# One pipeline for the state space and rotary stages, and another order of work in the latent attention

## The reference, cut to what matters

```python
# state space: a circulant map W (diagonal in Fourier space) steps the state
h_t = W h_(t-1) + B_w u_t              # u = layernorm(x)
x   = x + C_w h_t + D * u
# last layer, on x' = layernorm(x):
h   = x' + attention(rms_norm(x', norm1_w))    # rope on its input, causal softmax
x   = x + h + moe(rms_norm(h, norm2_w))        # router: top 2 of 8 experts
def rope(v):                                    # cos, sin by position in the sequence
    xe, xo = v[..., 0::2], v[..., 1::2]
    return concat([xe * cos - xo * sin, xe * sin + xo * cos])
```

## Time and profile before

| what | us |
|---|---|
| median of the runs (of 3, 1023.49 to 1028.31) | 1025.85 |
| the profiled execution, its own time | 1029.01 |
| its span, first to last instruction | 1027.2 |
| PE busy in the span | 787.1 |
| DVE busy | 540.1 |
| POOL busy | 439.3 |
| ACT busy | 428.7 |

### The profile page before, as it was taken

The page is one execution under the profiler, slowest core; times in us unless marked ns, Lnnn a source line. Parts: engine busy times, 40 slices in busy tenths (PEclk is TensorE's granted clock), DMA queues, the critical chain, the costliest instruction groups (busy, mean ns, idle before and its releaser), DMA issues.

```text
span 1027.2 us, 21336 instructions
## 1 busy us (share of the span) xinstructions
PE 787.1 (77%) x7200; PEld 574.0 (56%) x7200; DVE 540.1 (53%) x1413; ACT 428.7 (42%) x1491; POOL 439.3 (43%) x637
## 2 busy tenths in 40 slices
PE   2899997799789477999966526776545999999980
PEld 1677775688644135777744315564432566666660
DVE  3477876468644345788865764765231323322323
ACT  1577775256524124676651023666102333333320
POOL 4566663525377768777733343354350000000005
PEclk9899999789889788999996756876557999999995
DMA  8322225613332545554410003132392065152004
GB/s 277 144 73 77 78 59 190 217 48 110 99 123 73 185 131 169 168 168 136 145 42 0 0 0 123 43 97 89 106 379 72 27 236 179 38 197 87 17 22 123
DMA packets 66198, 116.82 MB, mean 114 GB/s; under 512 B 6576, under 2 KB 22704, under 8 KB 65456
## 3 DMA queue, kind: packets, MB, share of 16 engines
q1 hardware_dynamic: 57936, 105.25, 31.0%
q10 hardware_dynamic: 6624, 6.03, 1.8%
q0 software_dynamic: 1536, 4.20, 1.3%
HBM read 81.11 MB, written 34.34 MB: 112 GB/s over the span
## 4 chain that ended last, share of the span: by engine, by line
PE 51%; DVE 16%; POOL 10%; ACT 9%; issue 8%; DMA 4%; ACTq 0%; SPq 0%; DVEq 0%; POOLq 0%; another core or an unknown queue 0%
ACT probs L1208 6%; PE ps L622 5%; PE ps L1046 4%; PE ps L1047 4%; PE ps L1048 4%; PE ps L638 3%; PE ps L520 2%; PE ps L662 2%; PE ps L1069 2%; PE ps L1071 2%; PE ps L1070 2%; PE ps L522 2%; PE ps L521 2%; DVE probs L1712 2%; PE ps L1058 2%
## 5 line engine op out<-in xcount | busy, mean ns | idle before, releaser
L1393 POOL TENSOR_TENSOR piece_out<-piece_in,piece_out 128x512 f16<-128x512 f32 x96 | 117.0, 1219 | 7.7
L1611 POOL DMA_INDIRECT pt<-y_rows,neg x16 | 15.3, 959 | 233.3 <-DMA y_rows<-vbuf 228.7
L2145 DVE TENSOR_TENSOR probs<-ps,ctx_t 128x512 f32<-128x512 f32 x46 | 29.6, 686 | 154.0 <-PE ps L1048 154.0
L1358 POOL TENSOR_TENSOR var<-mv,half 128x1 f32<-128x1 f32 x48 | 9.3, 194 | 186.1 <-DVE mv L1627 114.3
L622 PE MATMUL ps<-pack_const,probs 128*128 128x128 f32 x512 | 75.4, 281 | 4.6 <-issue 3.1
L1392 POOL CAST piece_out<-piece_in 128x512 f16<-128x512 f32 x96 | 62.7, 653 | 24.0 <-DMA piece_in<-in_w 23.5
L1046 PE MATMUL ps<-arena,qbuf 128*128 x184 | 70.7, 384 | 0.0
L1047 PE MATMUL ps<-arena,qbuf 128*128 x184 | 70.5, 383 | 0.0
L1048 PE MATMUL ps<-arena,qbuf 128*128 x184 | 70.3, 382 | 0.0
L622 PEld LDWEIGHTS ps<-pack_const,probs 128*128 128x128 f32 x512 | 58.0, 143 | 21.1 <-issue 15.0
L1149 ACT ACTIVATE probs<-probs,mx 128x256 f32<-128x256 f32 x128 | 63.1, 498 | 6.9 <-DVE mx L1712 6.9
(11 more groups left out here) (286 smaller groups left out, 2192.8 us busy)
## 6 DMA issues: line engine op xcount, KB each, us to landing
piece_in<-in_w SPq DMA_DIRECT2D x96, 256.0 KB, 2.9
w_parts<-piece_out SPq DMA_DIRECT2D x96, 256.0 KB, 2.1
arena<-w_parts SPq DMA_DIRECT2D x8, 3072.0 KB, 12.8
ctx_t<-in_ctx SPq DMA_DIRECT2D x32, 256.0 KB, 2.9
x_rows<-piece_out SPq DMA_DIRECT2D x1, 2944.0 KB, 17.7
qbuf<-x_rows ACTq DMA_DIRECT2D x23, 128.0 KB, 2.1
y_rows<-vbuf ACTq DMA_DIRECT2D x23, 128.0 KB, 1.7
arena<-in_xa SPq DMA_DIRECT2D x2, 1282.0 KB, 7.8
```

Source lines behind the costliest of these rows:

```text
L1393: pool.tensor_tensor(both[:, PIECE:], src, both[:, 0:PIECE], ALU.subtract).then_inc(piece_split, 1)
```

## The change

- `ssm` and `rope` become one pipeline without a hardware loop. PE takes tile `k-4` of `rope` behind tile `k-2` of `ssm`. The scaling, the four products and the joining of `rope` move from DVE to POOL (`multiply`, `join_turns`), with `norm1` multiplied into the tables once. The root is no longer applied to the rows: ACT writes a diagonal matrix of it (`root_diagonal`), and the transposing product on PE is made with that matrix in place of the identity.
- D * u is no longer computed on POOL: ACT writes a diagonal of D, and PE adds two products of `XT` with it into the same PSUM tile (`read_out`). `keep_rows` and the copy into `xs` go away. PSUM tiles of the stage are doubled.
- `la` gets its own order on every engine, four slots for values, and `row_maxima` waits for the transposes of the tile whose buffer it overwrites.
- The router's products of tile `k-5` are made inside the steps of `la` (`route_rows`).

The diff, cut to its core:

```diff
-                    hold(pe, g["pt_copied"], 2 * (i - 2) + 1)
+                    hold(pe, g["pt_copied"], 2 * (i - (2 if st == "sa" else 3)) + 1)
...
+                def route_rows(i):
+                    if i == 0:
+                        pe.wait_ge(*loaded["moe"])
+                    hold(pe, g["xt"], i + 1)
+                    hold(pe, g["shifted"], at_most(i + 5, TILES))
+                    for c in range(DC):
+                        last = pe.matmul(S[:, 768 + i * 8:768 + (i + 1) * 8], tile_of_x(i, c),
+                                         kc(W["moe"]["router_w"], 8)[:, c, :], start=c == 0, stop=c == DC - 1)
+                    if i == TILES - 1:
+                        last.then_inc(prep_mm, 1)
...
+                for k in range(INNER_STEPS if st == "la" else 0):
+                    if live(k, 3, TILES):
+                        mix_values(k - 3)
+                    if live(k, 0, TILES):
+                        project(k)
+                    if live(k, 3, TILES):
+                        join_heads(k - 3)
+                    if live(k, 5, TILES):
+                        route_rows(k - 5)
+                    if live(k, 0, TILES):
+                        values(k)
+                        score(k)
+                    if live(k, 2, TILES):
+                        turn_probs(k - 2)
+                    if live(k, 4, TILES):
+                        turn(k - 4)
...
-                def project(i, s):
-                    hold(pe, g["x_copied"], i + 1)
-                    hold(pe, g["rotated"], i)
...
+                def read_out(i):
                     hold(pe, g["modulated"], i + 1)
-                    hold(pe, g["resid"], i)
+                    hold(pe, g["resid"], i - 1)
+                    if i == 0:
+                        pe.wait_ge(d_spread, 2)
                     for c in range(DC):
-                        last = pe.matmul(M[:, 256:512], rot2[:, s * D + c * P:s * D + (c + 1) * P],
-                                         kc(cg[:, :], D)[:, c, :], start=c == 0, stop=c == DC - 1)
+                        pe.matmul(state_out[i % 2], rot2[:, (i % 2) * D + c * P:(i % 2) * D + (c + 1) * P],
+                                  kc(cg[:, :], D)[:, c, :], start=c == 0, stop=False, skip_group_check=True)
+                    for c in range(DC):
+                        last = pe.matmul(state_out[i % 2][:, c * P:(c + 1) * P], XT[:, c, i * P:(i + 1) * P],
+                                         d_diagonal[:, c * P:(c + 1) * P], start=False, stop=True, skip_group_check=True)
                     last.then_inc(g["projected"].sem, 1)
-                def step(k, s, h):
+                def turn_rope(i):
+                    r = G["rope"]
+                    hold(pe, r["roped"], i + 1)
+                    hold(pe, r["weighed"], i + 1)
+                    hold(pe, r["xt"], i)
+                    for c in range(DC):
+                        last = pe.matmul(C[:, c * P:(c + 1) * P], rope_rows[i % 2][:, c * P:(c + 1) * P],
+                                         root_diagonal[i % 2], start=True, stop=True)
+                    last.then_inc(r["turned"].sem, 1)
...
+                for k in range(TILES + 4):
                     if live(k, 1, TILES):
-                        sum_over_time(k - 1, 1 - s)
+                        sum_over_time(k - 1)
                     if live(k, 0, TILES):
-                        project(k, s)
+                        project(k)
                     if live(k, 2, TILES):
-                        out(k - 2, s)
-                skewed(pe, TILES, 2, step)
-            if "rope" in RUN:
-                g = G["rope"]
-                def step(k, s, h):
-                    hold(pe, g["roped"], k + 1)
-                    hold(pe, g["xt"], k)
-                    for c in range(DC):
-                        last = pe.transpose(C[:, c * P:(c + 1) * P], rot[:, c * P:(c + 1) * P], ident)
-                    last.then_inc(g["turned"].sem, 1)
-                skewed(pe, TILES, 0, step)
+                        read_out(k - 2)
+                    if live(k, 4, TILES):
+                        turn_rope(k - 4)
...
+                for k in range(INNER_STEPS if st == "la" else 0):
+                    if live(k, 1, TILES):
+                        exps(k - 1, range(HEADS))
+                    if live(k, 2, TILES):
+                        copy_probs(k - 2)
+                    if live(k, 3, TILES):
+                        square(k - 3)
                     if live(k, 4, TILES):
-                        i = k - 4
-                        hold(act, g["turned"], i + 1)
-                        act.activation(XT[:, :, i * P:(i + 1) * P], C[:, 256:512].rearrange("p (c n) -> p c n", c=DC),
-                                       ACT.Copy).then_inc(g["xt"].sem, 1)
-                        if st == "la":
-                            act.activation(row_parts[i % 2][:, (i // 2) * 2 * D:(i // 2) * 2 * D + D], xn[:, :], ACT.Copy)\
-                               .then_inc(g["row_hi"].sem, 1)
+                        copy_rows(k - 4)
+                        take_high(k - 4)
...
+                def multiply(i):
+                    hold(pool, g["normed"], i + 1)
+                    hold(pool, r["roped"], i)
+                    pairs = tile(xn_all, i).rearrange("p (n a) -> p n a", a=2)
+                    for j, odd in enumerate((0, 1, 0, 1)):
+                        last = pool.tensor_tensor(xs[:, j * P:(j + 1) * P], pairs[:, :, odd], rope_tables[:, j * P:(j + 1) * P],
+                                                  ALU.mult)
+                    last.then_inc(r["multiplied"].sem, 1)
+                def join_turns(i):
+                    hold(pool, r["multiplied"], i + 1)
+                    hold(pool, r["turned"], i - 1)
+                    rows_out = rope_rows[i % 2]
+                    pool.tensor_tensor(rows_out[:, 0:P], xs[:, 0:P], xs[:, P:2 * P], ALU.subtract)
+                    pool.tensor_tensor(rows_out[:, P:2 * P], xs[:, 2 * P:3 * P], xs[:, 3 * P:4 * P], ALU.add)\
+                        .then_inc(r["roped"].sem, 1)
+                for k in range(TILES + 4):
+                    if live(k, 3, TILES):
+                        multiply(k - 3)
+                    if live(k, 3, TILES):
+                        hold(pool, r["weighed"], k - 4)
+                        inverse_root(r, k - 3, 2, mv[:, 0:1], "squared", "rooted", rstd2[:, (k - 3) % 2:(k - 3) % 2 + 1])
                     if live(k, 2, TILES):
-                        root_of_variance(g, k - 2)
+                        i = k - 2
+                        inverse_root(g, i, 1, mv_pair[:, 2 * (i % 4) + 1:2 * (i % 4) + 2], "stats", "rstd",
+                                     rstd_pair[:, i % 4:i % 4 + 1], omega)
+                    if live(k, 3, TILES):
+                        join_turns(k - 3)
...
+                    if st == "la":
+                        hold(dve, g["p_turned"], 2 * i - 2)
...
+                for k in range(INNER_STEPS if st == "la" else 0):
+                    if live(k, 1, TILES):
+                        sum_values(k - 1)
+                        row_maxima(k - 1, (k - 1) % 2)
+                    if live(k, 3, TILES):
+                        gather_outputs(k - 3)
+                    if live(k, 0, TILES):
+                        copy_queries_and_keys(k)
+                    if live(k, 2, TILES):
+                        scale_probs(k - 2, k % 2)
+                    if live(k, 3, TILES):
+                        add_heads(k - 3)
+                    if live(k, 4, TILES):
+                        scale_rows(k - 4)
+                    chain.restart()
```

233 lines of the change are left out of this document (107 added, 126 removed).

## The result

Four runs of the changed kernel have a median of **979.63 us** (979.10 to 981.45), four of the kernel before beside them 1027.05 us (1023.49 to 1028.31): a ratio of **0.9547, 95% interval 0.9518 to 0.9576**. The forecast was 984.0 in 974 to 1001. The profiled execution of the changed kernel took 979.1 us, with a span of 977.0; the span before was 1027.2, so the profiles differ by 50.2 us.

A forecast was written before the change was run, and what follows sets the result against it. No engine was full; rings of waits between engines, one per tile, and a second rotary pass bounded the kernel. Gains of 12.4 and 29.5 us made 41.9, from 1029.0 to 987.1, less 3.2 for the median: 984, range 974 to 1001.

The forecast's parts named there:

- The start does not move.: First pipeline: PE's first product still waits behind the two copied phase rows, so the stage opens when it did before.
- 6.7 per full step, five steps, +3.3: First pipeline: DVE's waits for POOL's SBUF lock add 0.7 us to each step of 6.05, over five steps.
- POOL's price, 0.5 per operation of 128x128: First pipeline: each new POOL product or joining takes 0.5 us with its gap, ends 0.25 and 0.73.
- The rival of a POOL that sets the pace: First pipeline: POOL operations cost 0.73 us, so 8.0 us per tile and 993 us in all; chance 0.10.
- The root of the last tile: +1.7.: First pipeline's end: the last root queues on POOL behind products and the previous tile's root, 1.7 us later.
- Gain of the first pipeline, 12.4: State space and rotary stages: PE begins queries and keys at 606.6 instead of 619.0, 12.4 us earlier.
- Opening of the attention, 28.6: Latent attention up to the fourth tile's values: 6.6 to the first values, 12.0 for two steps, 10.0 for the fourth.
- Steps, 9.2 at full clock: Latent attention: four steady steps of 9.2 us, DVE the bound, PE at full clock; ends 8.5 and 12.0.
- Close, 26.6: Latent attention, last values to logits: 35.7 us less 6.1 for the router's products and about 3 for tile 7's outputs.
- about 3 less: Attention's close: tile 7's outputs no longer stand behind tile 6's rows `xn`, which waited for POOL; about 3 us.
- The half clock: Rival, latent attention: PE stays at half clock, steady steps and the fourth cost 2.6 us more each, 997 us; chance 0.17.
- Weights late: Rival, experts' start: it hangs on the last weight piece, not the logits, giving back the router's 6.1; 990 us; chance 0.04.

The follow-up runs named there:

- all_tails: Changed kernel with last-tile reorderings: probabilities scaled and turned earlier, POOL's root before the products, POOL's low part of rows before its sum; 983.08 us, ratio 0.9578.
- pe_extra: Changed kernel with the values' products of every tile of the latent attention made twice on PE; 985.52 us, one run.

## Why the prediction was right, and where not

The forecast was 4.4 us above the median, inside the range. The sum hid larger errors of opposite sign. Of the 50.2 us between the two profiles it had 41.9: 8.2 too little in the first pipeline, 3.3 too much in the attention, nothing of the 5.2 of the opening, and not the 1.8 given back in the rest. That the median came out only 4.4 away is in part luck: the forecast also took off 3.2 because the first profile was slower than its median. The mechanism was right for the second pass that went away and for the router, and wrong for what sets the step in either stage.

- **"The start does not move."** Right for all that can be told: the 5.2 us between the first two profiles come from PE's clock in the first layer's experts.
- **"6.7 per full step, five steps, +3.3": wrong, 5.63.** Two terms failed. The locks were put at 0.7 us from POOL's share of the time; measured, one output in four waits, 0.27, and the normalise, which had paid 0.30 to 0.57 before (0.42 on the mean), pays 0.12, since POOL's operation beside it is 0.46 long and no longer 0.73. And the rolled loop's cost in the kernel before, 0.35 per step on the mean and 3.2 in all, was not seen at all, though the 0.33 us between two DVE operations of one step are in its trace (568.14, `L1639`).
- **POOL's price, 0.5 per operation of 128x128:** right, 0.46 and 0.50. The rival of a POOL that sets the pace fell for the steps; POOL does set the close.
- **"The root of the last tile: +1.7."** The wait was there (2.41, of which 0.93 is every step's), but it cost nothing, as `all_tails` showed: POOL was the bound there.
- **Gain of the first pipeline, 12.4: it was 20.6.** 7.7 of the 8.2 too little lay ahead of the end of the last normalise (58.7 predicted from the first phase turn, 51.0 measured): 5.4 in the five full steps and 1.9 in the opening, which the sum took over unchanged. The terms listed behind the last normalise (2.0, 0.8, 1.0 and 1.3) end at 606.3 and not at 606.6, a slip of 0.3.
- **Opening of the attention, 28.6:** 29.2. **Steps, 9.2 at full clock:** 9.0 at 1.00. The size is right, the reason is not: "DVE as the bound". `pe_extra` shows the ring through PE and ACT's copies; PE's products took 7.3 us of a step and not the 8.0 that I estimated, but the wait for those copies, 1.2 to 1.3, was left out.
- **Close, 26.6: wrong, 30.1.** The step that failed is "about 3 less": the rows of tile 6 did leave the path of the outputs of tile 7, but the mixing of tile 7 still waits for the transposed rows of tile 5, at half clock. With the router late the close took 34.8 against 35.7 before, so the 3 were 0.9; and the router's 6.1 were 4.7 in the close.
- **The half clock,** the main rival: it did not hold in the steps, but in the opening (0.78) and in the close (0.61). **Weights late:** in part. 1.8 us came back behind the logits, where POOL's last piece now ends 1.7 us late and the scattered rows land among the loads: a third of the price that I had set on it. That the piece is the cause was not tested.
